# Causal attention in one megakernel: value pieces issued in pairs, whole-array units directly behind them, maxima only between score pieces

## The reference

```python
def _L0_attn_ref(x, Wq, Wk, Wv):          # x (8, 1024, 256), W* (16, 256, 16)
    q = jnp.einsum('bte,hed->bhtd', x, Wq)
    k = jnp.einsum('bte,hed->bhtd', x, Wk)
    v = jnp.einsum('bte,hed->bhtd', x, Wv)
    scores = jnp.einsum('bhtd,bhsd->bhts', q, k)
    causal = jnp.tril(jnp.ones((T, T), dtype=bool))
    scores = jnp.where(causal, scores, -jnp.inf)
    scores = scores / jnp.sqrt(jnp.asarray(E, dtype=scores.dtype))
    w = jax.nn.softmax(scores, axis=-1)
    out = jnp.einsum('bhts,bhsd->bhtd', w, v)
    return jnp.transpose(out, (0, 2, 1, 3)).reshape(B, T, -1)
```

## Time and profile before

| | |
|---|---|
| median of 3 runs | 4440.13 us |
| profiled execution's own span | 4440.5 us |
| TensorE (PE) busy, whole span | 4192.7 us (94%) |
| VectorE (DVE) busy, whole span | 2790.9 us (63%) |
| ScalarE (ACT) busy, whole span | 2654.5 us (60%) |
| reduces of the maxima, L648 | 1280, 738.3 us |
| exponentials, L550 | 768, 584.1 us |
| matmuls of the value pieces, L501 | 3072 records, 332.9 us |

### The profile page before, as it was taken

The page is one execution under the profiler, slowest core; times in us unless marked ns, Lnnn a source line. Parts: engine busy times, 40 slices in busy tenths (PEclk is TensorE's granted clock), DMA queues, the critical chain, the costliest instruction groups (busy, mean ns, idle before and its releaser), DMA issues. The chain is left out here.

```text
span 4440.5 us, 62548 instructions
## 1 busy us (share of the span) xinstructions
PE 4192.7 (94%) x22580; PEld 2203.7 (50%) x22580; DVE 2790.9 (63%) x5566; ACT 2654.5 (60%) x3193; POOL 1452.8 (33%) x1111
## 2 busy tenths in 40 slices
PE   7999999999978999999999999998899999999999
PEld 4444444544535565565565565555344444444443
DVE  6777777777748677676676645554455554555553
ACT  2555555555556454454454423444688888888888
POOL 3111111111125343343343322221354544545545
PEclk7999999999999999999999999999899999999999
DMA  7333433433210000000000001000766667667673
GB/s 176 89 94 74 102 74 81 95 96 80 60 56 1 0 1 1 1 1 1 1 1 1 1 8 26 1 1 1 166 143 161 152 143 164 149 153 162 141 162 90
DMA packets 145746, 322.79 MB, mean 73 GB/s; under 512 B 39296, under 2 KB 64272, under 8 KB 129056
## 3 DMA queue, kind: packets, MB, share of 16 engines
q1 hardware_dynamic: 137456, 310.88, 30.5%
q10 hardware_dynamic: 7920, 7.87, 0.6%
q0 software_dynamic: 64, 0.05, 0.0%
HBM read 237.93 MB, written 80.74 MB: 72 GB/s over the span
## 5 line engine op out<-in xcount | busy, mean ns | idle before, releaser
L2108 ACT ACTIVATE gelu_out<-hidden,b_col 128x1024 f32<-128x1024 f32 x1024 | 1084.4, 1112 | 164.6 <-PE hidden L2008 163.8
L648 DVE TENSOR_REDUCE maxima<-front 128x1 f32<-128x512 f32 (+3 forms) x1280 | 738.3, 631 | 170.7 <-PE front L458 97.2
L2090 POOL TENSOR_TENSOR combined<-combined,gated 128x512 f32<-128x512 f32 x480 | 619.6, 1291 | 666.9 <-DVE gated L2205 458.9
L550 ACT ACTIVATE probsT<-scoresT 128x1024 f32<-128x1024 f32 (+3 forms) x768 | 584.1, 811 | 306.1 <-PE scoresT L486 301.6
L1061 POOL TENSOR_TENSOR pair_sums<-sims 128x1024 f32<-128x1024 f32 x256 | 481.9, 1903 | 784.5 <-DVEq L1187 516.7
L2205 DVE SCALAR_TENSOR_TENSOR gated<-expert_out,b_col,gates_spread 128x512 f32<-128x512 f32 x480 | 360.1, 750 | 501.9 <-PE expert_out L2018 296.2
L2008 PE MATMUL hidden<-slice_stack,w_stack 128*128 128x512 f32 x2048 | 628.0, 428 | 15.0 <-ACT gelu_out L2108 15.0
L2018 PE MATMUL expert_out<-gelu_out,w_sb 128*32 128x512 f32 x4096 | 548.6, 608 | 24.9 <-DVE gated L2205 13.5
L2008 PEld LDWEIGHTS hidden<-slice_stack,w_stack 128*128 128x128 f32 x2048 | 352.4, 189 | 371.8 <-ACT gelu_out L2108 283.1
L399 POOL TENSOR_SCALAR_AFFINE_SELECT probsT<-probsT 128x512 f32<-128x512 f32 x256 | 163.3, 638 | 1075.4 <-ACT probsT L550 1075.4
L452 PE MATMUL front<-k_stack,q_stack 62*128 62x512 f32 (+3 forms) x1536 | 434.8, 427 | 34.6 <-DVE maxima L648 14.7
(11 more groups left out here) (203 smaller groups left out, 5663.0 us busy)
## 6 DMA issues: line engine op xcount, KB each, us to landing
gates_spread<-gate_scratch SPq DMA_DIRECT2D x512, 256.0 KB, 4.9
stack_scratch<-split_parts SPq DMA_DIRECT2D x192, 256.0 KB, 3.0
slice_stack<-slice_scratch SPq DMA_DIRECT2D x128, 256.0 KB, 8.1
q_stack<-stack_scratch SPq DMA_DIRECT2D x64, 384.0 KB, 6.2
k_stack<-stack_scratch SPq DMA_DIRECT2D x64, 384.0 KB, 9.2
slice_scratch<-slice_parts SPq DMA_DIRECT2D x32, 512.0 KB, 6.4
out_x<-x_tiles ACTq DMA_DIRECT2D x15, 512.0 KB, 4.8
x_tiles<-in_L_attn_x SPq DMA_DIRECT2D x7, 1024.0 KB, 12.3
```

What stands on the lines that cost most here:

```text
L550: nc.scalar.activation(PT[:, i % NPT, 2 * pr:2 * pr + 2, at:BANK], ST[pr][:, :, at:BANK], ACT.Exp, scale=SCALE).then_inc(probs_ready, 1)
L648: nc.vector.tensor_reduce(dst, F[k % 3][:, 0:parts * w].rearrange("p (a k) -> p a k", a=parts), AX.X, ALU.max)\
L2090: nc.gpsimd.tensor_tensor(CM[:, par, hc, :], CM[:, par, hc, :], Y[:, u % 2, :], ALU.add)\
L2108: nc.scalar.activation(GH[:, k % 4, :, :], HP[k % HPB][:, :, :], ACT.Gelu, bias=b1c[:, u % E:u % E + 1])\
```

## The change

`step(n)` is rewritten. It goes through the tiles by twos: four score pieces (i and i + 1), then the two value pieces i - 2 and i - 1, then o where a chunk begins. The units of `spread`, and the t units that follow certain pairs of maxima, are held until a v or o is followed by a score piece, and put there. The pairs of maxima are put only ahead of a score piece (also behind the held units), not between two value pieces and not before whole-array units. How many are put is set by `load_of` as before. The units are the same ones; the 2688 entries of the list are only in another order.

```diff
--- before.py
+++ after.py
@@ -159,10 +159,10 @@
 
 
         pieces = []
-        for i in range(NG * n, NG * (n + 1)):
-            pieces += [("s", i, 0), ("s", i, 1)]
+        for i in range(NG * n, NG * (n + 1), 2):
+            pieces += [("s", i, 0), ("s", i, 1), ("s", i + 1, 0), ("s", i + 1, 1)]
             if i >= LAG:
-                pieces.append(("v", i - LAG))
+                pieces += [("v", i - LAG), ("v", i + 1 - LAG)]
                 if GROUPS[(i - LAG) % NG][2] == 0 and i > LAG:
                     pieces.append(("o", phase(i - LAG) - 1))
         spread = []
@@ -174,33 +174,33 @@
         if n:
             spread.append((0.07, ("t", n, 1)))
         spread.sort(key=lambda a: a[0])
-        whole = sum(pe_time(u) for u in pieces if u[0] in "sv")
-        rest, spent = [], 0.0
-        for u in pieces:
-            while spread and spread[0][0] * whole <= spent:
-                rest.append(spread.pop(0)[1])
-            rest.append(u)
-            if u[0] in "sv":
-                spent += pe_time(u)
-        rest += [u for _, u in spread]
-
         units = (maxima(0, 1)[EARLY:] if n == 0 else []) + maxima(n + 1, 0) + maxima(n + 1, 1)
         pairs = [units[k:k + 2] for k in range(0, len(units), 2)]
         turn_after = {len(pairs) - 20 + 3: ("t", n + 1, 0)} if n + 1 < NS else {}
         if n == 0:
             turn_after[len(pairs) - 40 + 3] = ("t", 0, 1)
-        whole, spent = sum(load_of(u) for u in rest), 0.0
-        all_pairs, done, k = sum(pair_load(p) for p in pairs), 0.0, 0
-        out = []
-        for u in rest:
+
+        out, late, k = [], [], 0
+        whole, at_whole = sum(pe_time(u) for u in pieces if u[0] in "sv"), 0.0
+        work = sum(load_of(u) for u in pieces) + sum(load_of(u) for _, u in spread)
+        all_pairs, done, spent = sum(pair_load(p) for p in pairs), 0.0, 0.0
+        for u, after in zip(pieces, pieces[1:] + [None]):
             out.append(u)
             spent += load_of(u)
-            while k < len(pairs) and (done + pair_load(pairs[k]) / 2) * whole <= spent * all_pairs:
-                out += pairs[k]
-                done += pair_load(pairs[k])
-                k += 1
-                out += [turn_after[k]] if k in turn_after else []
-        return out + [u for pair in pairs[k:] for u in pair]
+            at_whole += pe_time(u) if u[0] in "sv" else 0.0
+            if u[0] in "vo" and (after is None or after[0] == "s"):
+                while spread and spread[0][0] * whole <= at_whole:
+                    late.append(spread.pop(0)[1])
+                out += late
+                spent += sum(load_of(w) for w in late)
+                late = []
+            if after is None or after[0] == "s":
+                while k < len(pairs) and (done + pair_load(pairs[k]) / 2) * work <= spent * all_pairs:
+                    out += pairs[k]
+                    done += pair_load(pairs[k])
+                    k += 1
+                    late += [turn_after[k]] if k in turn_after else []
+        return out + late + [u for _, u in spread] + [u for pair in pairs[k:] for u in pair]
 
     def phase(i):
         n, (g, c, _) = i // NG, GROUPS[i % NG]
```

## The result

The changed kernel takes 4961.72 us, the median of 4 runs (4960.59 to 4962.83), against 4440.68 (4440.07 to 4442.83) for the kernel before in the same job: a ratio of 1.1174, 95% interval 1.1158 to 1.1189. The forecast was 4645 with a range of 4490 to 4745. The sign was right; the loss is 521 us where 205 were forecast.

What follows compares the result with a forecast made beforehand. TensorE was taken to bound the causal stage, coupled with VectorE through three `front` banks. Odd steps +89, even +91, step 0 +15, step 14 +7 and step 15 +3, together +205 on 4440 us, gave 4645; range 4490 to 4745.

Steps and rivals of the forecast that it cites:

- rival 4: Causal stage: the walk is right and TensorE's granted clock falls to 0.96, +40 us, 4685 us; 12 in 100.
- The range's upper end, 4745: Whole kernel: if the new order falls short by 8% like the old, the sum is about +305 us.
- the walk: Causal stage: unit durations and bank waits followed through the new order; odd steps +12.7 us, even +15.2, together +205.
- the walk's own trial: Step 9, old order, value pieces 4 to 8: the same rules gave 16.3 us against 17.8 in the trace.
- weight loads of `front` wait over 300 us for maxima: TensorE in the causal stage: waits for VectorE to empty `front` banks grow from 172.8 to over 300 us.
- wait for `scoresT` would at least double: TensorE in the causal stage: waits for ScalarE to empty `scoresT` banks at least double from 68.0 us.
- VectorE's busy time would not grow: Causal stage: VectorE's busy time stays near 878 us plus a little, its idle time grows to some 30 per step.
- Step 15: Causal stage's step without maxima: ScalarE bounds it; 4.8 us for a full pair, 4.5 before, +3 us in all.
- The saved changes: TensorE, causal stage: 658 fewer switches of how its array is used, at 0.09 us each, 59 us less.
- DMA: Stores of q and k parts from three buffers: costed at nothing; if not covered, some 1 us per step.
- the stages behind: Everything after the causal stage, from about 1280 us on: unedited, must keep its old lengths.

Runs made afterwards that it cites:

- four issues: The changed kernel with the first matmul of each maximum issued four times: 5013.53 us, ratio 1.1291.
- the run with two issues: The changed kernel with the first matmul of each maximum issued twice: 4842.53 us, ratio 1.0905.
- both readers quick: VectorE's reduces cut to 128 columns and ScalarE's exponentials to 128 queries, in the changed kernel (4454.64 us) and in the kernel before (4320.60 us).
- pairs alone: The kernel before with only four score pieces then two value pieces, maxima and whole-array units spread as before: 4646.95 us, ratio 1.0448.
- slots alone: The kernel before with only the pairs of maxima moved to directly ahead of score pieces: 4614.74 us, ratio 1.0391.

## Why the prediction was wrong

- **The term that failed** is the clock: at nothing in the sum that gives 4645, and in rival 4 "the granted clock falls besides, from 0.99 to the 0.96 that the last step has", at +40 us. It fell to 0.76 and costs some 327 us by the estimate above. I had seen the condition for it, "TensorE stands still more often in the new order", and then priced it with 0.96, the lowest clock among my rows of the trace before, as if it bounded what a different order could do. That row had TensorE busy 37 of 42 us, a share of 0.89; the changed kernel's step 9 has 0.91 and a clock of 0.70. The busy share doesn't tell the clock, and a matmul at 1.2 GHz raises that share itself. The range's upper end, 4745, came from the walk alone and held nothing for it.
- **The walk** (+205 in all) comes close to what is left. At nearly full clock, with four issues, steps 1 to 13 last 1474.0 / 13 = 113.4 us; less three issues at 7.9 (1083.2 - 980.6 = 102.6, over 13; 980.6 is before's) and less 0.06 x 113.4 x 0.41 = 2.8 for the clock, that is 86.9, and by the same working 88.0 from the run with two issues. Before it is 75.4, and the walk had 88.7. This rests on each issue costing as much here as in the order before. Step 9 alone comes out at 84.6 where the walk had 85.5. The nearness is in part luck. With both readers quick, where the walk's rules leave little but the splits and the 59 us saved, the new order is still some 93 us behind without the clock (134 less 41), so a part of the 197 is something that the walk does not hold. Nor had the walk's own trial, 8% short on the old order, been put into the forecast; it would have made it 4745.
- **Where the waits would show** was wrong. I had "weight loads of `front` wait over 300 us for maxima"; it was 121.8. I had put the loss on the pace of the reduces. The parts show two losses of like size (205 and 173 us): the two score pieces more before the value pieces, which wait for ScalarE (pairs alone), and the maxima in fewer places (slots alone). That the wait for `scoresT` would at least double was right (68.0 to 162.9), and so was that VectorE's busy time would not grow (871) and its idle time would: 58.0 us of step 9, not 30.
- **Step 15**, forecast at +3, came out at +15.4 (42.0 to 57.4 from its second value piece to its last output). It has no maxima; in the changed order with short exponentials it takes 36.2, with pairs only 54.5. I had counted ScalarE's work per round and no wait of TensorE behind it, and there, too, the clock fell, to 0.79.
- **The saved changes**, -59 us: one row bears them out (1.64 us for a pair at full clock, where 0.09 us more inside it would make 1.77), and they show in no total. In the pair of kernels meant to bare them, both readers quick, the new order is 134 us slower. Of these, the 99 us at 1.2 GHz account for some 41 by the estimate; the rest, and the 59 that should have come back, stay open. That the doubled and held blocks put work in series which lay side by side before is argued, not shown.
- **DMA and the stages behind** at nothing: right for the latter (3156 against 3160 us). For the three buffers of stored parts no run tells it apart.

## What to carry to other kernels

Where TensorE's order is dense and many engines empty its banks, a saved change of the array's use pays only if nothing is bunched by it: the change is 0.09 us here, and each bunching of short matmuls or of one engine's work that was run lost more than it saved. Price an order that adds short waits twice, with TensorE at 2.4 and at 1.2 GHz, since two rearrangements that cost 205 and 173 us alone cost 476 together, and the surplus was the clock; and don't bound the lower clock by the lowest row of a trace that hardly had it (31 of 1181 us). Whether the clock is the cause is best asked with redundant matmuls in both orders: where more work makes the new order faster and the old one slower, the clock is the first suspect, and its records show whether it came back. To see where it falls, look at what TensorE did in the few us ahead of each fall: here it was stretches without value pieces, and with waits.

## What the runs showed of the hardware

- The clock falls with no long stop of TensorE: in step 9 after, at a granted clock of 0.70, it is busy 103.2 of 113.5 us, and the longest time without a matmul in it is 2.1 us (4.3 in the whole stage). 48% of the stage ran at 1.2 GHz. The Trainium skill (TensorE: Matmul & The Clock Gate, A second HAM failure mode) describes short idle stretches between groups of matmuls that make the clock swing; this case agrees, and adds a size, by the estimate 327 us of 4962.
- Redundant matmuls paid: 1 more issue per maximum, 119 us less in all. With three more the clock was at 0.97, but the work cost more than it brought back.
- The clock falls in stretches of maxima and score pieces with short waits (no value piece in the 3 us ahead of 90 of 105 falls, TensorE at a stand for 28% of that time), and value pieces behind them, which never stop, are paid at half speed: 358 of their 445 us. The waits count besides the order of the units: the same order with both readers quick has 20 falls. Whether missing value pieces alone, without waits, would lower the clock no run here shows.
